# First-pass score units of the next sequence one slot nearer to the front of the step

## The reference, cut to what matters

```python
x = L0_attn_x                      # (32, 256, 128)
xn = _layernorm(x, axis=-1)
x = x + _L0_attn_ref(xn, ...) + _L0_ffn_ref(xn, ...)

# _L0_attn_ref
scores = jnp.einsum('bhqd,bhkd->bhqk', q_rot, k_rot) / jnp.float32(math.sqrt(dh))
scores = scores + decay_bias[None]
scores = jnp.where(causal[None, None], scores, jnp.float32(-jnp.inf))
attn = jax.nn.softmax(scores, axis=-1)
out = jnp.einsum('bhqk,bhkd->bhqd', attn, v)

# _L0_ffn_ref: gates from n1 and smha_sim, then
q = jnp.einsum('btc,ech,bte->bth', n1, q_proj, rw)
k = jnp.einsum('btc,ech,bte->bth', n1, k_proj, rw)
v = jnp.einsum('btc,ech,bte->bth', n1, v_proj, rw)
attn = jnp.einsum('bts,bsh->bth', jax.nn.softmax(scores, axis=-1), v)
attn_out = jnp.einsum('bth,ehc,bte->btc', attn, o_proj, rw)
```

## Time and profile before

| | |
|---|---|
| median of 3 runs | 1577.72 us (1576.56 to 1579.24) |
| the profiled execution | 1577.96 us, span of its instructions 1576.2 us |
| busy in the span: PE, PEld, DVE | 1338.6, 1024.4, 1081.8 us |
| busy in the span: ACT, POOL | 815.0, 341.4 us |
| TensorE busy from 200 to 1180 us | 914.9 of 980 us, full granted clock |
| a step, from one first second-pass unit to the next (653.53 to 688.12) | 34.59 us |

### The profile page before, as it was taken

How to read it: one execution, slowest core, us unless ns; L and a number is a source line. 1 busy time by engine, 2 the same in 40 slices (tenths; PEclk the granted TensorE clock), 3 DMA queues, 4 the chain that set the end, 5 groups by cost and what they waited for, 6 DMA issues and landing times.

```text
span 1576.2 us, 34759 instructions
## 1 busy us (share of the span) xinstructions
PE 1338.6 (85%) x10534; PEld 1024.4 (65%) x10628; DVE 1081.8 (69%) x4153; ACT 815.0 (52%) x1752; POOL 341.4 (22%) x422
## 2 busy tenths in 40 slices
PE   1289999999899999999999999999994588888887
PEld 0157777777777777777777777777773355555555
DVE  7567766777777667777776777777634577777771
ACT  1136556566655566666556566665662344444342
POOL 3011221111122111111221111112111233333332
PEclk9689999999999999999999999999997699999999
DMA  4413323222233232322333322233200333223332
GB/s 108 96 45 77 79 73 100 74 78 69 68 82 76 76 99 68 79 68 72 80 75 85 89 77 70 69 79 79 75 34 10 115 135 127 102 107 134 133 135 81
DMA packets 86696, 133.21 MB, mean 85 GB/s; under 512 B 9163, under 2 KB 77115, under 8 KB 77371
## 3 DMA queue, kind: packets, MB, share of 16 engines
q1 hardware_dynamic: 86098, 132.10, 29.5%
q10 hardware_dynamic: 488, 0.01, 0.0%
HBM read 108.76 MB, written 21.50 MB: 83 GB/s over the span
## 4 chain that ended last, share of the span: by engine, by line
PE 54%; DVE 18%; ACT 11%; issue 9%; DMA 4%; DVEq 1%; SPq 1%; POOL 1%; ACTq 0%; POOLq 0%
PE ps L1363 6%; PE ps L1364 5%; PE ps L1408 5%; PE ps L1373 5%; PE ps L1572 4%; PE ps L1341 4%; PE ps L1237 3%; DMA qst<-mT 3%; PE ps L1322 3%; ACT pr L651 2%; DVE ats L1164 2%; PE ps L1299 2%; PE ps L1564 2%; PE ps L1292 2%; PE ps L1295 1%
## 5 line engine op out<-in xcount | busy, mean ns | idle before, releaser
L651 ACT ACTIVATE pr<-ps 128x512 f32<-128x512 f32 x384 | 227.2, 592 | 176.6 <-PE ps L1322 155.7
L1007 DVE TENSOR_REDUCE mx<-ps 128x2 f32<-128x512 f32 (+1 forms) x384 | 264.2, 689 | 49.8 <-PE ps L1299 26.8
L515 POOL TENSOR_TENSOR n1s<-rep,n1T 128x256 f32<-128x256 f32 x256 | 176.9, 729 | 292.5 <-PE ps L1373 274.7
L656 ACT ACTIVATE ps<-trn 128x512 f32<-128x512 bf16 x382 | 229.7, 601 | 12.1
L1572 PEld LDWEIGHTS ps<-w2s,ats 128*128 128x128 f32 x1024 | 127.3, 191 | 91.7 <-DVE ats L1164 47.8
L1572 PE MATMUL ps<-w2s,ats 128*128 128x128 f32 x1024 | 140.3, 280 | 34.2 <-DVE ats L1164 26.6
L522 POOL TENSOR_TENSOR zt<-xn,rstd 128x256 f32<-128x256 f32 x32 | 19.6, 612 | 655.2 <-DVE rstd L849 655.2
L1363 PE MATMUL ps<-n1s,wq 128*128 128x256 f32 x512 | 159.8, 394 | 0.0
L783 ACT ACTIVATE n1s<-ps 128x512 f32<-128x512 f32 x128 | 76.4, 597 | 156.5 <-PE ps L1564 155.1
L1364 PE MATMUL ps<-n1s,wk 128*128 128x256 f32 x512 | 152.7, 380 | 0.0
L1373 PE MATMUL ps<-wv,n1s 128*128 128x128 f32 x1024 | 150.6, 280 | 0.0
(11 more groups left out here) (222 smaller groups left out, 2482.2 us busy)
## 6 DMA issues: line engine op xcount, KB each, us to landing
rep<-scr_rw SPq DMA_DIRECT2D x32, 1024.0 KB, 5.1
qst<-scr_rw SPq DMA_DIRECT2D x8, 2048.0 KB, 7.5
kst<-scr_rw SPq DMA_DIRECT2D x8, 2048.0 KB, 7.5
scr_parts<-parts SPq DMA_DIRECT2D x64, 192.0 KB, 2.3
qst<-scr_parts SPq DMA_DIRECT2D x192, 64.0 KB
kst<-scr_parts SPq DMA_DIRECT2D x32, 192.0 KB
xt<-in_x SPq DMA_DIRECT2D x32, 128.0 KB, 2.3
kst<-scr_parts SPq DMA_DIRECT2D x32, 128.0 KB
```

The source lines that it names most:

```text
L515: pool.tensor_tensor(n1s[:, e], rep[:, par, e], n1T[:, par], ALU.mult).then_inc(n1s_done, 1)
L651: act.activation(pr[:, G % 2, i], ps[:, S2[k % 2]], ACT.Exp).then_inc(exp_done, 1)
L656: act.activation(ps[:, S2[k % 2]], seeds[:, 1 if (k + 2) % 3 == 2 else 0], ACT.Copy).then_inc(seed_done, 1)
L1007: dve.tensor_reduce(mx[:, min(i, 1), h:h + n], ps[:, S1[k % 2]].rearrange("p (h t) -> p h t", h=n), AX_X, ALU.max, negate=True).then_inc(s ...
```

## The change

On TensorE the first unit of the first pass gets a new place, behind the first `qk` of the step. Every other unit moves to the slot that its predecessor had, and slot 11, behind `soft_T`, goes. On VectorE the first reduction moves ahead of the rotation, every other one to the place that its predecessor had, and the last place, behind the gates, goes. ScalarE, GpSimd and SyncE keep their lists. The waits inside the units are as before.

```diff
                 def beside_rotation(k):
                     if k in (1, 3, 5):
-                        next_max((1, 3, 5).index(k))
+                        next_max(1 + (1, 3, 5).index(k))
...
                     if k in GATE_MAX_AT:
-                        next_max(4 + GATE_MAX_AT.index(k))
+                        next_max(5 + GATE_MAX_AT.index(k))
...
+                next_max(0)
                 if n_x >= 2:
                     rotate(n + 2, beside_rotation)
-                    next_max(3)
+                    next_max(4)
                     gating(n + 2, T, 0, gate1, beside_gating)
                     run(norm)
...
-                next_max(11)
                 if n_x:
                     max_parts(n + 1)
...
                 qk(n, 0)
+                next_max(0)
                 unit2(n, u, 1)
...
                 qk(n, 1)
-                next_max(0)
+                next_max(1)
                 unit2(n, u, 2)
...
                 ve(n, 2)
-                next_max(10)
+                next_max(11)
                 unit2(n, u, 11)
                 ve(n, 3)
                 soft_T(n)
-                next_max(11)
                 ve(n, 4)
                 pv(n, u, 3)
```

More of the change, by code:

```diff
@@ L1449, in step @@
                     proj(f, 1, lambda: pe.wait_ge(rot_chain, ROT_LINKS * f + 1))
-                next_max(1)
+                next_max(2)
                 unit2(n, u, 3)
@@ L1455, in step @@
                 pv(n, u, 0)
-                next_max(2)
+                next_max(3)
                 unit2(n, u, 4)
                 qk(n, 4)
-                next_max(3)
+                next_max(4)
                 unit2(n, u, 5)
                 qk(n, 5)
-                next_max(4)
+                next_max(5)
                 unit2(n, u, 6)
                 pv(n, u, 1)
-                next_max(5)
+                next_max(6)
                 qk(n, 6)
-                next_max(6)
+                next_max(7)
                 unit2(n, u, 7)
@@ L1470, in step @@
                 qk(n, 7)
-                next_max(7)
+                next_max(8)
                 unit2(n, u, 8)
@@ L1476, in step @@
                 ve(n, 0)
-                next_max(8)
+                next_max(9)
                 pv(n, u, 2)
@@ L1480, in step @@
                 ve(n, 1)
-                next_max(9)
+                next_max(10)
                 unit2(n, u, 10)
                 ve(n, 2)
-                next_max(10)
+                next_max(11)
                 unit2(n, u, 11)
```

## The result

The changed kernel takes 1584.79 us (median of 7 runs, 1583.00 to 1587.44) against 1577.50 us (7 runs) for the kernel before: a ratio of 1.0048 with a 95% interval of 1.0034 to 1.0062, 7 us slower. In the profiled executions the span grew from 1576.2 to 1583.0 us.

The account below looks back on a forecast made before the run. TensorE's instructions plus stalls were taken to bound the attention step. Transposes 3.4 us plus the maxima's DMA 6.6 us made 10.0 us slower, added to the 1577.7 us median for 1587.7 us; range 1575.5 to 1592.5 us.

Parts of the forecast that it names:

- The frame: TensorE in the attention phase: the change adds and removes no work and can only move stalls between waiting partners.
- Term 2: First second-pass unit's wait for the maxima DMA: landing 0.33 us later against its reader, mean 0.22 us, 6.6 us slower.
- served in the order of its code: SyncE's queue: the stack data's tail stands ahead of the maxima DMA, tying its landing to the stack DMAs' start.
- Term 1: Stall at the soft-max transposes: start 0.44 us later, 0.33 us saved behind, 0.11 us in 31 steps, 3.4 us slower.
- VectorE's row moves by 0.44 us too: Steps whose soft-max chain comes through VectorE: the reduction ahead of the rotation's work ends later, shifting that row 0.44 us.
- What costs nothing: Step's start: the first unit's new place and its reduction cost nothing, its input issued earlier and VectorE idle there.
- (a): Maxima DMA's landing hangs on its own issue and latency: 0 to 3.4 us slower, 1577.7 to 1581.1 us; chance 0.21.
- (b): Stall at the soft-max transposes absorbs the last first-pass unit: 0.33 us gained per step, 10.2 us, 1567.5 us; chance 0.13.
- (c): First first-pass unit waits for its stacks near the step's start: at most 1.95 us per step, 1636 us; chance 0.06.

Follow-up runs that it names:

- the split: Each stack DMA cut in two by heads, the first half issued earlier: on the kernel before 1566.08 us, on the changed kernel 1569.12 us.
- the small k: The three DMAs filling the stacked k cut to one row each: on the kernel before 1562.15 us, on the changed kernel 1564.99 us.
- moving U9: Changed kernel with stack DMAs split by heads, and the tenth first-pass unit put directly behind the tenth second-pass unit: 1562.49 us, ratio 0.9901.
- the front half alone: Kernel before with only the first five first-pass units one slot earlier, slot 4 empty, reductions moved alike: 1573.24 us, ratio 0.9985.
- the late: Kernel before with the stack DMAs also waiting for the soft-max transposes, TensorE's list untouched: 1639.29 us, ratio 1.0378.

## Why the prediction was right, and where it was off

**The frame held.** Nothing was added or removed, and the time changed by what the order does to two pairs of partners. The sum of 10.0 us measured 7.3 us by the medians, 7.6 us by the ratio (0.0048 x 1577.5).

**Term 2, the DMA of the maxima.** 0.22 us a step, 6.6 us, was expected. In the two profiled executions the mean step grew by 0.30 us, and by 0.07 to 0.08 us where the wait is taken away (the pairs with the split and with the small k), which leaves 0.22 to 0.23 us. The medians of all runs give less: 7.3 us between the two kernels and 3.0 or 2.8 us between the pairs leave 4.3 or 4.5 us, 0.15 us a step, uncertain by some 2.5 us. So the size was near, and in part by luck, for the shift that it is made of was mis-sized: 0.33 us was worked out, and in the steps shown 0.25 and 0.09 us were lost in turn, 0.17 us on average. The 0.33 us took for granted that all steps shift alike. In the pair with the split, the last second-pass unit comes 0.44 us later in the steps that grow by 0.17 us, which leaves 0.27 us; in the others, which don't grow, that unit comes only 0.09 us later. Against this, more steps paid than I took: the list has 9 waiting steps, the starts have 13 of 27, and 22 after the change. The listed idle time went from 4.2 to 8.2 us, where about 10 was named.

The mechanism was right in what the landing is tied to, the start of the stack data, and wrong in how: "served in the order of its code" isn't what makes the maxima late. They are about as late on ScalarE's queue. I inferred queue order from 189 KB still moving behind the issue. These show that data is moving, not that the order in one queue is the reason; the two had to be parted by an experiment. How the moving data holds the maxima back stays open. In the changed kernel's step shown, the DMA engines are at work until some 0.9 us ahead of the reader's start at 690.37:

```profile
688.50:689.50 1.00, 1.00 (x12) 1.00 (x11) 0.00 (x0) 0.00 (x0) 0.13 (x1) 1.00 0.15 30
689.50:690.30 0.80, 0.36 (x4) 0.13 (x2) 0.60 (x2) 0.32 (x2) 0.00 (x0) 1.00 0.00 0
```

Their mean busy share is only 0.15 in the last stretch with data, and the views don't tell single engines apart.

**Term 1, the stall at the transposes.** 0.11 us in each step, 3.4 us, was too much: 0.07 to 0.08 us, and 2.8 to 3.0 us between the pairs. The step that failed is "VectorE's row moves by 0.44 us too" for the steps in which the chain goes through VectorE. The row's start did move by 0.44 us, but it became shorter inside. Before, from the start of the rotation's remainder to that of the negated maximum, it took 639.60 - 628.32 = 11.28 us; in the same step of the changed kernel, by VectorE's timeline,

```profile
630.84 0.68 DVE L935 TENSOR_TENSOR rres<-rot,parts 128x512 f32<-128x512 f32 x1
...
641.74 0.17 DVE L1043 TENSOR_SCALAR smx<-smx 128x2 f32<-128x2 f32 x1
```

it takes 10.90 us. Compared row by row the two are alike to 0.03 us, but for one place between two small links of the first rsqrt. Before:

```profile
632.88 0.16 DVE L99 TENSOR_TENSOR vstd<-vstd 128x4 f32<-128x4 f32 x1
633.35 0.16 DVE L96 SCALAR_TENSOR_TENSOR gs<-gs 128x2 f32<-128x2 f32 x1 [0.31 <-issue]
```

and in the changed kernel:

```profile
635.38 0.16 DVE L99 TENSOR_TENSOR vstd<-vstd 128x4 f32<-128x4 f32 x1
635.49 0.16 DVE L96 SCALAR_TENSOR_TENSOR gs<-gs 128x2 f32<-128x2 f32 x1
```

The gap of 0.47 us has become one of 0.11. What made it, and why it went, I haven't tested. With this VectorE's row is no longer the bound in these steps. In the kernel before ScalarE's soft-max exp (L671) started at 639.81, as soon as the maximum was there; in the changed kernel the maximum is ready at 641.91, and the exp follows 0.29 us later, behind ScalarE's own row:

```profile
642.20 0.35 ACT L671 ACTIVATE sp<-ps,smx 128x128 f32<-128x128 f32 x1
```

So these steps, every second one, lost nothing: undisturbed they are 34.57 us before, and 34.57 after (the pair with the split). The others, bound by ScalarE in both kernels, lost 0.49 - 0.33 = 0.16 us (34.39 to 34.57), for which 0.11 was worked out; of this, 0.05 us arise before the gated scores (0.38 in place of 0.33) and stay unexplained. That ScalarE's row starts with the tenth unit's exp, and that it is the length of U9 ahead of it that counts, is shown by moving U9: 6.6 us, 0.20 us a step.

**What costs nothing** was right and too careful: the front half alone gains 2 to 3 us. Its steps that VectorE bounds take 34.45 us undisturbed, where they took 34.57; they have one reduction less ahead of the soft-max maximum.

**The rivals.** (a), that the landing hangs on its own issue, is refuted by the late and by the small stacks. (b), that the stall at the transposes absorbs the unit, failed as argued: the stall grew from 0.71 to 0.79 us in the steps shown. (c), that U0 waits for its stacks, is refuted by the changed kernel's own trace, and the front half's: no wait ahead of L1288 or L1292 for a DMA appears, although U0 comes 1.1 us behind the first second-pass unit (656.23 - 655.14). (In the prediction, 3.2 us is the distance of U0's mask, at 656.76; its score matmuls at 656.98 stood 3.45 us behind. The price worked out is that of the mask and stands.)

**Open:** the prologue and the first three steps are 1.5 us shorter in the changed kernel's profile. In the pairs they are longer instead, by 1.6 us with the split and 2.1 us with the small k, and I made no experiment on them. That they are a gain of the new order isn't shown.

## What to carry to other kernels

When a change only shifts work along a full engine, list the partners that wait on both sides of each stall and shift each by the length of what moved past it; unequal lengths (0.44 against 0.33 us) and a tail that moves less than the start of a transfer are what costs or gains. Do this for each kind of step: where two rows bind in turn, the shift that one of them gets can be lost in the slack of the other. A transfer whose landing has no slack should be traced back to when the bulk ahead of it started, not only to when it was issued; here it was worth more to start that bulk earlier, in pieces (11 us), than to give the transfer another queue (nothing that can be measured). Here the best of the splits and orders together gave 1%, where the slot change alone cost half a percent.

## What I had not expected of the hardware

A small DMA (24 KB) was as late on another engine's queue as behind 768 KB on the same one: 1576.6 against 1576.4 us. And delaying the start of this data by 1.8 us cost 2.1 us a step: the wait itself grew by about the delay, and in 7 of 26 steps it was long enough that TensorE came back from it at half its clock and lost another 1.5 us.
